# Expert stage: which weight matrix the load queue asks for next

## The reference

```python
probs = jax.nn.softmax(xt @ Wr + br, axis=-1)
top_p, top_idx = jax.lax.top_k(probs, 2)
weights = top_p / top_p.sum(axis=-1, keepdims=True)
xe = xn[None, :, :] * ln_g[:, None, :] + ln_b[:, None, :]
h = jax.nn.gelu(jnp.einsum('end,edh->enh', xe, W1) + b1[:, None, :], approximate=False)
y = jnp.einsum('enh,ehd->end', h, W2) + b2[:, None, :]
out = (weights[:, :, None] * sel).sum(axis=1)     # sel: the two chosen experts' rows of y
```

## Time and profile before

| what | value |
|---|---|
| runs | 2354.43 us median of 3 (2350.54 to 2369.11) |
| profiled execution | 2361.64 us, span from first to last instruction 2359.9 us |
| granted clock of TensorE, mean of the span | 0.846 |
| busy: PE, DVE, ACT, POOL | 1735.6, 1451.0, 727.5, 1545.0 us |

### The profile page before, as it was taken

One profiled execution on the slowest core, in us unless ns is written; L12 is line 12 of the kernel. 1 busy time (PEld: TensorE's weight loads), 2 busy tenths in 40 slices (PEclk: granted clock), 3 DMA queues, 4 the chain that ended last, 5 costly groups with the idle time before them and its releaser, 6 DMA issues.

```text
span 2359.9 us, 38011 instructions
## 1 busy us (share of the span) xinstructions
PE 1735.6 (74%) x12869; PEld 1383.5 (59%) x12869; DVE 1451.0 (61%) x3795; ACT 727.5 (31%) x1607; POOL 1545.0 (65%) x1009
## 2 busy tenths in 40 slices
PE   2655544477777777677777777179589999999997
PEld 1333333345454544466566665178478888888886
DVE  2789977778778875233333333069866666666664
ACT  1011111144444444211111111047344433334432
POOL 2888888888888888888888888810034444545442
PEclk9676655579999999688888888589699999999999
DMA  9987777765555444555555554365538888878885
GB/s 301 234 181 172 146 154 151 145 103 75 70 69 75 69 69 69 81 74 78 74 85 79 73 85 65 37 167 168 185 98 271 252 252 244 271 240 259 254 268 157
DMA packets 401454, 348.00 MB, mean 147 GB/s; under 512 B 39304, under 2 KB 323531, under 8 KB 401261
## 3 DMA queue, kind: packets, MB, share of 16 engines
q1 hardware_dynamic: 268492, 266.72, 35.7%
q0 software_dynamic: 132768, 78.84, 28.6%
HBM read 236.69 MB, written 108.76 MB: 146 GB/s over the span
## 4 chain that ended last, share of the span: by engine, by line
PE 27%; DMA 26%; POOL 26%; issue 11%; DVE 7%; SPq 2%; ACT 0%; POOLq 0%; DVEq 0%; ACTq 0%
POOL node_table L1535 25%; DMA node_table<-edge_sums,row_i 19%; PE bank L730 10%; PE bank L744 8%; DMA big<-w_parts 6%; PE bank L687 2%; DVE hotB L871 2%; PE bank L699 1%; PE bank L701 1%; PE bank L522 1%; PE bank L679 1%; DVE hotA L868 1%; SPq L1584 1%; PE bank L716 1%; PE bank L482 1%
## 5 line engine op out<-in xcount | busy, mean ns | idle before, releaser
L1535 POOL DMA_INDIRECT node_table<-edge_sums,row_i x782 | 1256.2, 1606 | 278.9 <-issue 206.4
L482 PE MATMUL bank<-edge_rows,same_node 128*128 128x129 f32 x1564 | 293.0, 336 | 209.3 <-ACT edge_sums L1333 109.0
L1333 ACT COPY edge_sums<-bank 128x387 f32<-128x387 f32 (+1 forms) x261 | 125.0, 479 | 1044.1 <-DMA node_table<-edge_sums,row_i 749.6
L482 PEld LDWEIGHTS bank<-edge_rows,same_node 128*128 128x128 f32 x1564 | 250.5, 238 | 256.8 <-issue 228.1
L1561 POOL DMA_INDIRECT result<-mixw,edge_rows x105 | 167.6, 1596 | 307.1 <-DVE mixw L1290 150.1
L1487 ACT ACTIVATE mixw<-bank,edge_rows 128x256 f32<-128x256 f32 (+1 forms) x456 | 242.7, 550 | 354.9 <-PE bank L730 244.4
L730 PE MATMUL bank<-edge_rows,big 128*128 128x256 f16 (+1 forms) x2736 | 296.9, 269 | 21.6 <-DMA big<-w_parts 20.7
L730 PEld LDWEIGHTS bank<-edge_rows,big 128*128 128x128 f16 x2736 | 251.8, 99 | 61.6 <-DMA big<-w_parts 26.3
L744 PE MATMUL bank<-big 128*128 128x256 f16 x2520 | 284.4, 273 | 1.0 <-issue 1.0
L504 PE MATMUL bank<-hotA,hotB 128*128 128x49 bf16 x1564 | 116.9, 200 | 203.4 <-DVE hotB L871 202.2
L1550 POOL DMA_INDIRECT state<-xn_rows,edge_rows x105 | 116.3, 1107 | 221.5 <-DVE edge_rows L1249 189.8
(11 more groups left out here) (283 smaller groups left out, 2516.9 us busy)
## 6 DMA issues: line engine op xcount, KB each, us to landing
big<-w_parts SPq DMA_DIRECT2D x114, 1024.0 KB, 7.1
edge_rows<-edge_attr SPq DMA_DIRECT2D x130, 384.0 KB, 3.7
big<-L_ffn_W SPq DMA_DIRECT2D x128, 128.0 KB
w_parts<-big SPq DMA_DIRECT2D x64, 256.0 KB, 3.5
node_table<-z_parts SPq DMA_DIRECT2D x20, 640.0 KB, 7.4
node_table<-edge_sums,row_i POOLq DMA_INDIRECT x782
mixw<-node_table SPq DMA_DIRECT2D x96, 128.0 KB, 2.4
edge_rows<-L_ffn_b SPq DMA_DIRECT2D x57, 128.0 KB, 8.1
```

What stands on the lines that cost most here:

```text
L482: ins = e.matmul(ps_sum[:, i * XW:(i + 1) * XW], S[:, g % SRING, i * P:(i + 1) * P], X[:, c // LOAD % XRING, c % LOAD, :], start=True, sto ...
L1535: e.indirect_dma_start(table[t], bass.IndirectOffsetOnAxis(ap=row_i[:, g % ORING, i:i + 1], axis=0), O[:, g % ORING, i, 0:RW], None, compu ...
```

## The change

The queue's list of loads is put in another order. `load_block` is cut into three functions, `load_up` (W1), `load_down` (W2) and `load_meta` (table and b2). Before the loop stand W1 and the table of block 0. Turn j of the loop issues W1 of block j+1, then W2 of block j, then the table and b2 of block j+1. Each function reads the expert's number itself, so that a block has three register loads in place of one. Every wait is the one that the same load had before; buffers, sizes and the four other engines' programs are the same.

```diff
-    def load_block(e, j):
+    def load_up(e, j):
+
         if j >= BLOCKS:
             return
-        r, c, m = j % 2, blocks[j][0], j % NM
+        r, c = j % 2, blocks[j][0]
         if j == 0:
             e.wait_ge(routed, ROUTE_OWNER)
             weights_stored(e)
@@
         which = e.value_load(owner_i[0:1, c:c + 1], min_val=0, max_val=EXPERTS - 1)
         e.dma_start(W1r[:, r].rearrange("p i k n -> p (i k n)"),
                     w_parts[0][bass.ds(which, 1)].rearrange("o p n -> p (o n)"), max_dma_last_dim=2048).then_inc(w1_load[r], 16)
+
+    def load_down(e, j):
+
+        r, c = j % 2, blocks[j][0]
+        which = e.value_load(owner_i[0:1, c:c + 1], min_val=0, max_val=EXPERTS - 1)
+        if j >= 2:
+            e.wait_ge(down_done, tiles_before[j - 1])
+        e.dma_start(W2r[:, r].rearrange("p i h n -> p (i h n)"),
+                    w_parts[1][bass.ds(which, 1)].rearrange("o p n -> p (o n)"), max_dma_last_dim=2048).then_inc(w2_load[r], 16)
+
+    def load_meta(e, j):
+        if j >= BLOCKS:
+            return
+        c, m = blocks[j][0], j % NM
+        which = e.value_load(owner_i[0:1, c:c + 1], min_val=0, max_val=EXPERTS - 1)
         if j >= NM:
...
-        if j >= 2:
-            e.wait_ge(down_done, tiles_before[j - 1])
-        e.dma_start(W2r[:, r].rearrange("p i h n -> p (i h n)"),
-                    w_parts[1][bass.ds(which, 1)].rearrange("o p n -> p (o n)"), max_dma_last_dim=2048).then_inc(w2_load[r], 16)
@@
         store_y(e)
+        load_up(e, 0)
+        load_meta(e, 0)
         for j in range(BLOCKS):
-            load_block(e, j)
+            load_up(e, j + 1)
+            load_down(e, j)
+            load_meta(e, j + 1)
```

## The result

The changed kernel takes **2331.68 us** in the median of six runs (2330.63 to 2337.3). The kernel before was run six times as well in the same comparison: 2360.2 us (2350.54 to 2369.11, the three runs of the prediction among them). The ratio is 0.988, with a 95% interval of 0.986 to 0.990: 28.5 us between the medians, 24 to 34 by the interval. A second comparison on another occasion gave 2326.03 against 2356.75, ratio 0.987 (0.985 to 0.989). So the kernel became about 1.2% faster. The forecast was 2322.

A forecast was written before the change was run, and what follows sets the result against it. PE was taken to bound the expert stage, transfers close behind. Waits and restarts 23.9, clock 7.8 and b2 0.9 make 32.6 us, taken from the 2354.4 us median to give 2322; range 2313 to 2345.

The forecast's parts named there:

- The sum, 32.6 us: Expert stage: 23.9 us of waits for W1, 7.8 of slow products and 0.9 of late b2 would go.
- waits 23.9: PE's up products waiting for W1: 20.7 us of idling and 20 restarts at 0.16 would go.
- clock 7.8: Four slow up products behind stalls, one of 8.22 us and three of 7.10, would go without the idling: 7.8 us.
- b2, 0.9 us: PE once waited for ACT, whose gelu waited for its table and b2; with b2 leaving earlier, 0.9 us gained.
- The rival at 0.14: b2 or a load is late next: 1.5 us at both narrow windows of 9 single blocks, 27 us; 2331 to 2349.
- W2, register loads, the table's wait: nothing: SyncE's queue: W2 behind W1, two more register loads a block (1.5 us) and the table's wait would cost nothing.
- The 13.9 us of room: W2's narrowest time until its down product needs it, in which even its longest landing, 12.0 us, fits.
- POOL's chain of adds: slower: Wait in `pool_add`: adds slowed by loads beside them become the bound; over 1% slower from x = 9.5; chance 0.07.
- the prediction's own formula: POOL's chain of adds takes 57x + 48 x 1.93 us, x being last add of a block to first of the next.
- Nothing changes, no room: W1 loads leave earlier but finish as before, DMA engines at 0.82, or a later resource holds; 2345 to 2358; chance 0.12.
- The rule of 2 us plus bytes at 436 GB/s: Transfer time by the Trainium skill: the pair of megabytes in 6.8 us after first issue, so the sum would be zero.
- the forecast's own 2314 to 2331: Execution time if all three terms come to nearly all, with the spread of runs; chance 0.67.

The follow-up runs named there:

- the filled stalls: The kernel before the change, with 16 small matmuls into an unused bank ahead of PE's waits that the single blocks cause; 2356.52 us, ratio 0.999.
- the kernel with W1, b2, W2 together: The changed kernel with W1 also waiting for the old pair's down product, and table and b2 issued before W2; 2330.45 us, ratio 0.990.

## Why the prediction was right

- **Bound and place.** PE's own work bounds the stage; the losses were W1 loads late at the single blocks. Shown: no wait for weights is left, and the changed kernel's stage doesn't change when the loads are taken away.
- **The sum, 32.6 us.** The stage fell by 32.3 us, to 566.3 against 566.0. Taken over both profiles of each kernel it is 30.0 to 32.9. Its parts were sized from one execution: waits 23.9 and clock 7.8 there, 27.3 and 3.1 in another. The clock term is real, as the filled stalls show, but its size is one execution's.
- **b2, 0.9 us.** Right, PE behind ACT lost 0.2 us after the change. But I took the short end of its landing (6.6) and the median was 6.7; what made that possible is the spacing, since with both megabytes close ahead b2 costs more than 20 us. The rival at 0.14 was the most real of the three: its 27 us stand beside the 24.0 that a late b2 cost where both megabytes left together, and the changed kernel avoided it by the distance of W1 from W2.
- **W1 earlier or W1 first?** The prediction named both and didn't part them. By the stage, the order in the pair (with b2 between) is 27.2 us, the earlier issue 5.7.
- **W2, register loads, the table's wait: nothing.** Right: no down product of the changed kernel waits for W2. The 13.9 us of room hold for its issue times only; issued last of a pair and landing after up to 11.2 us, W2 was late once, by 0.6.
- **POOL's chain of adds: slower.** Refuted. The adds got no slower, 7.3 to 7.9 us against 8.5, and POOL's waits for them fell from 127.2 us to this (both from 1760 to 2320 us):

```profile
POOL result L1561 <- DMA result<-mixw,edge_rows: 60.6, 14, 8.5
```

  Why they got faster is not shown: with b2 ahead of W2 in the changed kernel the same stage of 565.7 us goes with 8.2 us. That the chain was near being the bound did not fall. By the prediction's own formula 8.5 us make 577, beside PE's 575, and in the kernel with W1, b2, W2 together (8.5 us in 47 places) VectorE did once wait for a buffer.
- **Nothing changes, no room.** Refuted by 322 GB/s with 0.2 us of waiting.
- **The rule of 2 us plus bytes at 436 GB/s.** By the Trainium skill, DMA: Bandwidth & Descriptors, Anatomy of one DMA, there was no wait to remove. The trace disagrees: removing the wait gave 32 us of the stage. The page gives the rule for transfers that GpSimd issues, and these are issued by SyncE, with other traffic beside them, so the prediction had stretched it.
- **The time.** 2322 against 2331.7. The mechanism was right; what was off is the base, the median of three runs (2354.4, where six have 2360.2), and 4 us between the stage's 32.6 and the 28.5 of the runs, which the interval (24 to 34) doesn't separate. In the second comparison the difference is 30.7, at 2326. The time lies inside the stated range, but 0.7 us above the forecast's own 2314 to 2331 and inside the first rival's 2331 to 2349; that it was not this rival is read from the waits and not from the time.

## What to carry to other kernels

A queue that serves several buffers in order delays each load to the latest condition ahead of it: list for every load when its buffer comes free and when its data is needed, put them in that order, and place a small late load ahead of the big ones where they leave together. Look for the narrowest window, which odd-sized blocks make, and treat the window behind it too, since a wait that is cured in one place alone can move to the next. The median of a few runs is no base to a few microseconds: a gain of 1% is better measured by a stage between two instructions than by the whole run.

## What the runs showed of the hardware, unexpected

- The granted clock fell after some short idle times and not after others: behind the first pair of ups, in the two profiles of the old kernel, slow products followed 4 of 5 waits of over 2 us (2.13 to 3.36), then 2 of 6 (2.37 and 3.20; 3.44 was followed by none).
- One core held 354 GB/s over 500 us with PE, ACT, DVE and POOL at work, above the 333 of the busiest short window before; the DMA share read 1.09 there, so a share near 1 was not the end.
- The shortest landing of a megabyte was 5.1 us; of two issued 1.2 us apart, as in the old order, the first took 5.4 us and the second 8.9 in the median; b2, 128 KB in 128 rows, landed after 5.1 to 8.6 us behind one of them (the changed kernel) and after up to 10.4 behind two.
- The first products of the stage have waits of some 2 us marked "issue" in some executions of either kernel, 4 to 6 us in all. Their cause stays open.
